# Graph network on one core: node numbers kept in SBUF, and ScalarE fetching a column in two rounds of three

## The reference

```python
q, k, v = ...                                  # layer 0, rows q|v of 128 floats gathered by src
scores = einsum(q[edge_src], k[edge_dst]) / 4
agg = segment_sum(softmax_by_dst(scores) * v[edge_src], edge_dst)
h_edge = (atom[src] + bond) @ W                # layer 1, rows of 64 floats
msg = leaky_relu(concat(h[src], eh) @ W_msg)   # layer 2, rows of 64 floats
h = relu(concat(x[src], e) @ msg_w1[l] + b)    # layer 3, after its own projection: rows of 128 floats
x = layernorm(x + layer(x, ...))
```

## Time and profile before

| | us |
|---|---|
| median of 3 runs | 14026.2 (14020.19 to 14042.77) |
| the profiled execution's own time | 14023.7 |
| its span, first to last instruction | 14022.0 |
| POOL busy | 6487.0 (46%) |
| DVE busy | 4894.6 (35%) |
| ACT busy | 3146.0 (22%) |
| SP's placements of layer 0, first to last (24) | 651.4 to 3118.5 |
| layer 1 (26) | 3715.0 to 6559.2 |
| layer 2 (26) | 7094.2 to 10112.4 |
| layer 3 (26) | 10738.9 to 13698.2 |

### The profile page before, as it was taken

How to read it: one execution, slowest core, us unless ns; L and a number is a source line. 1 busy time by engine, 2 the same in 40 slices (tenths; PEclk the granted TensorE clock), 3 DMA queues, 4 the chain that set the end, 5 groups by cost and what they waited for, 6 DMA issues and landing times. The chain is left out here.

```text
span 14022.0 us, 92846 instructions
## 1 busy us (share of the span) xinstructions
PE 2267.2 (16%) x11897; PEld 1811.0 (13%) x11897; DVE 4894.6 (35%) x6191; ACT 3146.0 (22%) x3841; POOL 6487.0 (46%) x6837
## 2 busy tenths in 40 slices
PE   2000000002000000000344433444432111111112
PEld 1000000001000000000244333433330000000002
DVE  3443333345444444445222222222242222222223
ACT  0221111114111111112132222332232222222222
POOL 6644444456544444444544444444434444444444
PEclk6555555555555555555677777777765555555556
DMA  6222222221222222222222222222212222222222
GB/s 239 81 73 70 74 70 74 70 90 34 63 66 65 65 70 68 65 65 81 61 79 78 71 77 80 79 79 71 77 44 68 70 67 72 72 72 72 71 71 69
DMA packets 418910, 1046.03 MB, mean 75 GB/s; under 512 B 198760, under 2 KB 226218, under 8 KB 403804
## 3 DMA queue, kind: packets, MB, share of 16 engines
q1 hardware_dynamic: 177424, 680.51, 13.0%
q0 software_dynamic: 219488, 334.23, 10.0%
q10 hardware_dynamic: 21612, 27.96, 0.6%
HBM read 633.14 MB, written 401.95 MB: 74 GB/s over the span
## 5 line engine op out<-in xcount | busy, mean ns | idle before, releaser
L982 POOL DMA_INDIRECT se<-x_table,edge_ix x1481 | 1400.8, 946 | 1855.7 <-DMA edge_ix<-in_src 815.7
L982 POOL DMA_INDIRECT hidden<-hidden_table,edge_ix x1468 | 1388.7, 946 | 1761.0 <-DMA edge_ix<-in_src 1289.8
L982 POOL DMA_INDIRECT g<-x_table,edge_ix x1468 | 1388.5, 946 | 1648.8 <-DMA edge_ix<-in_src 1169.1
L982 POOL DMA_INDIRECT qv<-qv_table,edge_ix x1443 | 1378.6, 955 | 1404.4 <-DMA edge_ix<-in_src 865.8
L1144 ACT ACTIVATE edge_sums<-edge_val 128x1904 f32<-128x1904 f32 (+3 forms) x220 | 1116.4, 5075 | 1084.9 <-issue 1050.9
L1837 DVE TENSOR_TENSOR edge_product<-mk_ps,edge_q_now 128x256 f32<-128x256 f32 x391 | 166.1, 425 | 2308.8 <-ACT edge_msg L1772 2262.0
L1134 DVE TENSOR_TENSOR_SCAN edge_val<-edge_bank,edge_val 128x464 f32<-128x464 f32 (+1 forms) x715 | 687.6, 1032 | 672.0 <-ACT edge_val L1940 441.6
L1932 PE MATMUL edge_e_ps<-w_nodes,edge_ea_t 128*128 128x512 f32 x784 | 476.6, 774 | 2733.9 <-DMA edge_ea_t<-in_edge_attr 1165.2
L1982 DVE TENSOR_TENSOR hidden<-hidden,edge_e_ps 128x3584 f32<-128x3584 f32 x55 | 213.8, 3888 | 1799.2 <-DMA hidden<-edge_sync_rows 1232.4
L1727 PE MATMUL mk_ps<-w_mk,edge_se_t 128*128 128x128 f32 x3128 | 523.1, 320 | 1656.6 <-issue 1399.5
L1087 ACT ACTIVATE edge_bank<-edge_weight_arg 128x112 f32<-128x112 f32 (+2 forms) x171 | 38.9, 228 | 2939.9 <-issue 1980.9
(11 more groups left out here) (463 smaller groups left out, 8657.6 us busy)
## 6 DMA issues: line engine op xcount, KB each, us to landing
edge_sync_rows<-x_table SPq DMA_DIRECT2D x6656, 0.2 KB
sums<-edge_sums SPq DMA_DIRECT2D x55, 1848.0 KB
sums<-edge_sums SPq DMA_DIRECT2D x55, 1792.0 KB
sums<-edge_sums SPq DMA_DIRECT2D x55, 1008.0 KB
edge_sync_rows<-hidden_table SPq DMA_DIRECT2D x3328, 0.5 KB
sums<-edge_sums SPq DMA_DIRECT2D x55, 924.0 KB
edge_k<-k_edges SPq DMA_DIRECT2D x56, 896.0 KB
edge_bond<-in_edge_attr SPq DMA_DIRECT2D x56, 896.0 KB
```

Source lines behind the costliest of these rows:

```text
L982: e.indirect_dma_start(self.gather_into(u, j), None, self.gather_from, bass.IndirectOffsetOnAxis(ap=now[:, j:j + 1], axis=0))\
```

## The change

All 1568 node numbers of each partition are loaded once in the prologue into `src_now` (it replaces a tile of three chunks), and POOL gathers from it; `index`, `index_in`, `load_index` and SP's waits for landed gathers go. ACT fetches column J - 2 in the second and third of each three rounds, into a pair of buffers, in six slots of 44, 44, 40, 44, 44 and 40 rows in the six chunks of three rounds. SP's loop and ACT's loop both hold three rounds. In layer 2 the tile `product` becomes two tiles of four columns each, used in turn.

```diff
-SCALAR_HELPS_SECOND = (0, 1, 3)
+SCALAR_HELPS = (0, 1, 3)
+CYCLE = 3
+SLOTS = ((0, 44), (44, 88), (88, P))
...
-            load(e, p.first_src[:, :], ins["src"][:, 0:3 * J])
+            load(e, p.src[:, :], ins["src"][:, :])
...
             for b in (0, 1):
-                for c in range(self.parts):
-                    self.wait_part(e, i, b, c, placed=False)
                 if b and self.sync_helps and not helped:
                     self.tell_last(e, i + 1)
-                if b and others is not None:
-                    hold(e, self.other_in, others, self.passed)
-                load_index(b, bass.ds(i * (2 * J) + (2 + b) * J, J))
                 hold(e, self.attr_free[b], at(i, 1, 1), self.passed)
                 load(b, i * 2 + (2 + b))
...
+                with e.Fori(0, whole) as k:
+                    turn(k * CYCLE + first, True, True, at(k, 16, 16 * (first + 1)))
+                    turn(k * CYCLE + (first + 1), True, True)
+                    turn(k * CYCLE + (first + 2), True, True)
...
+            both(r, lay=None if begins else (r, 1, at(k, 16 * P, 0), second), tell=16 * (first + 1) if begins else None,
+                 rows=((0, SLOTS[0], ready[0]), (0, SLOTS[1])))
+            both(r + 1, tell=at(k, 16, 16 * (first + 2)),
+                 rows=((0, SLOTS[2]), (1, SLOTS[0], ready[1]) if second else None))
+            both(r + 2, lay=(r + 2, 0, at(k, 16 * P, 16 * P), not ends),
+                 rows=((1, SLOTS[1]), (1, SLOTS[2])) if second else None)
...
                 if n >= len(self.gathered):
-                    e.wait_ge(self.index_in[b], 16 * i)
                     if self.begun and n in (3, 4):
...
+                    if last_alone and i:
+                        e.wait_ge(self.placed, 16 * i)
+                    if other_alone and i:
+                        e.wait_ge(self.laid, 16 * i)
...
-                e.tensor_tensor(product[:, now, :], mk_ps[u][:, :, FD:], q_now[u][:, :, :], ALU.mult)
+                e.tensor_tensor(product[u][:, :, :], mk_ps[u][:, :, FD:], q_now[u][:, :, :], ALU.mult)
```

More of the change, by code:

```diff
@@ L857, in by_scalar @@
     def by_scalar(self, i):
[L859 to L860 removed]
+        return self.scalar_helps and i in range(self.opening, self.rounds - 1) and (i - self.opening) % CYCLE > 0
     def fetch(self, e, rows, numbers, to, landed):
@@ L934, in scalar_rounds @@
-        quarter = P // 4
-        def two(i, k, tells, lays):
-            both(i, lay=(i, k, True) if lays else None, tell=None if lays else 16 * (first + 1),
-                 rows=(slice(0, quarter), slice(quarter, half)), ready=(i, k, lays))
-            both(i + 1, tell=tells, rows=(slice(half, half + quarter), slice(half + quarter, whole)))
-        pairs = (self.rounds - 2 - first) // 2
-        assert first + 2 * pairs == self.rounds - 2
-        two(first, 0, 16 * (first + 2), False)
-        with e.Fori(1, pairs) as k:
-            two(k * 2 + first, k, at(k, 16, 16 * (first + 2)), True)
@@ L946, in scalar_rounds, with cycle @@
-        both(self.rounds - 2, lay=(self.rounds - 2, pairs, False))
+        first = self.opening - 1
+        count = [len(range(first + 2 + u, self.rounds - 1, CYCLE)) for u in (0, 1)]
+        cycles = count[0]
+        for u in (0, 1):
+            self.load_numbers(e, first + 2 + u, 1, self.at_scalar[u], self.at_scalar_in[u])
+        for i in range(first):
+            both(i, tell=16 * (i + 1))
+        def cycle(k, begins=False, ends=False):
+            r = k * CYCLE + first
+            laid = (None, None) if begins else (at(r, 16, 0), at(r, 16, 16))
+            ready = [(at(k, 16, 16), laid[u]) for u in (0, 1)]
+            second = not ends or count[1] == cycles
+            both(r, lay=None if begins else (r, 1, at(k, 16 * P, 0), second), tell=16 * (first + 1) if begins else None,
[4 more added lines that the diff above has]
+                 rows=((1, SLOTS[1]), (1, SLOTS[2])) if second else None)
@@ L948, in store_cut @@
+        cycle(0, begins=True)
+        with e.Fori(1, cycles - 1) as k:
+            cycle(k)
+        cycle(cycles - 1, ends=True)
+        if count[1] == cycles:
+            both(self.rounds - 2, lay=(self.rounds - 2, 1, 16 * P * cycles, False))
     def store_cut(self, e):
@@ L1433, in _, with both @@
             turn_k(0, 0, 0)
-            def both(i, lay=None, tell=None, rows=None, ready=None):
+            def both(i, lay=None, tell=None, rows=None):
                 if lay:
```

115 lines of the change are left out of this document (46 added, 69 removed).

## The result

The changed kernel takes 14126.8 us (median of 4 runs, 14111.1 to 14153.2), 1.0072 of the kernel before (95% interval 1.0054 to 1.0089): 0.7% slower, where 13,500 us and faster was forecast. The profiled execution has a span of 14123.4 us, 101.4 more than before.

A forecast was written before the change was run, and what follows sets the result against it. SP's turn, slowed by rows issued under POOL's gathers, was taken as the bound. Layers 0 to 3 gave -55 - 73 - 226 - 166 = -520 us from 14026, so 13,500 us; own range 13,250 to 13,730, wider range 13,130 to 13,930.

The forecast's parts named there:

- What bounds the kernel: All layers: SP's turn sets the round; rows issue at 2.1 us each under POOL's gathers, 0.32 us otherwise.
- POOL is freed from SP: POOL starts when its buffer is free, overlapping SP's non-row stretches: -226 us in layer 2, -4 us a round elsewhere.
- both buffers come free early: Layer 2: chunk (i+1, 1) can follow (i+1, 0) at once, giving a round of 112 us, -8.7 us a round.
- ACT's loop: Three rounds in ACT's loop body: 1.9 us a round charged for the jump back, bounds 0 and 1.9.
- ACT's rows: ACT issues 85 rows a round instead of 64; in layer 1 this uses up its 22 us of idle cover.
- layer 1 becomes ACT's: ACT sets layer 1's round at 111 us, between 104 and 118.5: -2.8 us a round, -73 us.
- SP's loop: SP's 5.7 us jump back is paid once in three rounds instead of two: -0.9 us a round.
- Layer 3: SP still sets the round, at 112 us against ACT's 104: -6.4 us a round, -166 us.
- The slower one: Rival: ACT's fetch becomes the bound in layers 0, 1 and 3; 124, 126 and 105 us rounds, 14,250 us; chance 0.11.
- mark of 60 us: The slower rival decides once ACT's half round passes 60 us; seen in layers 1 and 3, it would refute the forecast.
- The small gain: Rival: overlap gives nothing, only loads and loops stay; -210 us, 13,815 us; chance 0.18.
- The shared row engine: Rival: ACT's added rows slow SP by 6.7 us in 76 rounds, +509 us, 14,015 us; chance 0.05.

The follow-up runs named there:

- k10: Changed kernel with no single rows: SP and ACT fetch nothing, POOL gathers all 28 columns of every chunk; 11,389 us, 0.8115 of the kernel before.
- k1: Kernel before with node numbers resident and no index loads, ACT still fetching every second round; 14,190 us, 1.0111 of the kernel before.
- k8d: Changed kernel with ACT fetching nothing, POOL gathering that column in every round; 14,259 us, 1.0150 of the kernel before.
- k6b: Kernel before with resident node numbers, plus a semaphore letting POOL start a chunk only at SP's first row; 13,846 us, 0.9860 of the kernel before.
- k2: Changed kernel with node numbers loaded by chunk again, keeping ACT's fetching by threes and three-round loops; 14,127 us, 1.0068 of the kernel before.
- k5d: Changed kernel plus a semaphore letting POOL start a chunk only at SP's first row; 14,062 us, 1.0004 of the kernel before.
- k3: Changed kernel with SP's loop over rounds written out in layers 0, 1 and 3; 14,143 us, 1.0069 of the kernel before.
- k9: Changed kernel, unedited, on the other kind of chip; 8,842.3 us, 1.0059 of the kernel before.
- k4: Kernel before with SP's loop over rounds written out in layers 0, 1 and 3; 14,038 us, 1.0005 of the kernel before.
- k7: Kernel before, SP's loops of layers 0, 1, 3 written out, 128 idle SP instructions ahead of layer 2's loop; other kind of chip, 8,788.5 us, 0.9997.

## Why the prediction was wrong

- **What bounds the kernel.** SP's turn, and the two rates at which it issues rows: shown in layers 0, 1 and 3 by k10 (78 us without rows). In layer 2 this was wrong: with or without rows it is 119 to 123 us, a loop of POOL's stretch and TensorE's and ACT's work after it, of the same length as SP's turn by chance.
- **"POOL is freed from SP", -226 us in layer 2, -4 us a round elsewhere.** This is the step that failed first. It assumed that "both buffers come free early". They come free as late as the node numbers came (54 waits, 1387 us in layer 2, where it had been 1421); POOL's stretches in layer 2 stayed two, and the layer gained 30 us in the changed kernel and 34 in k1. Where the stretches did join (k8d), the rows became slower in layer 1, and in layers 0 and 3 SP waited for the sums in their place. The account moved POOL's 69 us about in slow and quick time freely. It left out that the removed waits had kept POOL's start beside SP's. Freed, POOL started by the time of its buffers, and SP was early or late: +7.8, +2.2 and +1.2 us a round in k1, and with a semaphore all of it and more came back (k6b). Why the phase settles where it does in each layer, layer 0 the worst, isn't shown.
- **ACT's loop, 1.9 us a round with bounds of 0 and 1.9.** This is the second step, a mis-sized term. ACT's jump back costs 11.5 us in layer 0 and 13.0 in layer 1, so 3.8 and 4.3 us a round. "Shows nothing such" was a wrong reading of the kernel before, where the jump lay in ACT's idle time.
- **ACT's rows.** That layer 1 becomes ACT's was right in mechanism: its cover was used up, its 44 rows took 44.6 us in the fetch shown (38.3 to 45.4 forecast), and the round is 116.0 us, between the bounds of 104 and 118.5 and 5 above the 111 that was taken. In layer 0, forecast at 105, ACT sets the round too, at 109.7. In both the loss sits there (+55 and +57 us). By itself fetching by threes costs 4.0 us a round in layer 0 and nothing in layers 1 and 3 (k2: -0.1 and -0.3 us), where ACT keeps idle time; in layer 1 ACT's fetch takes 41.2 us in the mean in the changed kernel, 35.4 in k2 and 32.8 in k5d, so there it takes both halves of the change to make ACT the bound.
- **SP's loop, 5.7 us per jump.** About right by its own measure, 6.3 us, and more to the first row. But k3 shows no gain without it, so the term was worth nothing.
- **Layer 3, forecast at -6.4 us a round and +1.6.** ACT has idle time there (11.6 us before its Relu copies, in the mean). SP's two fetches take 102.5 us in place of 100.9, and the rest of its turn is as long as before, so none of the three gains came.
- **The rivals.** The slower one named the right engine, ACT, and one of the right places, layer 1. But it kept layer 0 at 105 us, it put a large loss into layer 3, where ACT has idle time, and its reason, quick rows lost to SP and attributes that land late, isn't what the trace shows: ACT took 20 rows in the first 10 us of a stretch and SP 7. Its mark of 60 us for ACT's half round was not reached; 57.2 in the half shown were enough. The small gain had the right thought (the rows need their quick time wherever POOL's stretches lie) with the wrong sign. The shared row engine would have made k8d faster, and it was slower; in layer 1 of k5d SP and ACT issued 14 and 13 rows in the same 5 us. So the rule of the Trainium skill, DMA: Bandwidth & Descriptors, section "Issuing engines are not separate DMA queues", is not what made this loss.
- **Not seen at all:** that the rows themselves were the price. The earlier trace rows had it: POOL's 56 gathers are 70 us, and 128 rows at these rates are 96. To remove a helper is a question to be asked as well as to speed one up.

## What to carry to other kernels

A wait that looks idle may hold two queues in step: before removing it, ask when each of them will start afterwards, and not only that it may start earlier. Cost a helper against the engine it helps, at the rate the helper gets while that engine works. Look at every engine for the one without idle time, and count what its idle time had covered, a jump back among it, as soon as it is gone. And where an engine's waits vanish, name the next signal on the same instruction before counting any of them as gained.

## What the runs showed of the hardware

- The same kernel takes 14,030 us on one kind of chip and 8,790 us on another. On the first a row (256 or 512 bytes, one DMA) issued from SP or ACT while GpSimd gathers takes 2 to 2.5 us, on the second 0.36 us. The chips of the first kind had odd numbers and those of the second even ones; seven chips don't prove a rule, and the cause is open.
- On the first kind TensorE's chain in layer 2 moves slowly while GpSimd gathers (7.0 busy us of 32 in k10), held by two waits of ACT in each chunk (10.66 and 15.77 us in the one shown); in the same layer of k9, with GpSimd gathering all along, TensorE was busy for 40.3 of 62 us.
- At full rate SP and ACT hardly slow each other: 14 and 13 rows, or 16 and 13, in the same 5 us in k5d, where the earlier trace rows has 16 in 5.05 us and 15 in 4.9. Under the gathers each gets its own 2 rows in 5 us.
- A queue that starts its rows as GpSimd starts, or after it, gets quick ones first: SP 25 in 9.1 us when it starts 1.9 us behind (k6b), ACT 7 in 4 us even 17 us behind.
- ACT's jump back to the start of its loop took 11.5 us each time in layer 0 and 13.0 in layer 1, on SP 6.3 us from store to next load.
- SP's one-round loop of layer 2 drew 13 or 14 instruction packets in 25 rounds in some kernels and 134 or 135 in others (k4, k7, k5d), with 5.3 us and more in place of 1.2 from store to next load, and in k4 with 126.0 us a round in place of 120.7.
